# RWKV, experts and a gated recurrence on one core: weights from a surplus made once, sums by accumulating transfers, and a new order of the queues

## The reference

```python
# layer A: RWKV time mix, then channel mix (16 sequences)
k, v, r = (mix(xn, lx, m) @ w for m, w in (key, value, receptance))   # lx: xn shifted by one token
w = exp(time_decay)
# over the tokens, per channel; alpha = beta = 0, eps = -1e30
tau = max(u + k_t, eps); e1 = exp(eps - tau); e2 = exp(u + k_t - tau)
out_t = (e1 * alpha + e2 * v_t) / (e1 * beta + e2)
tau2 = max(eps - w, k_t); d1 = exp(eps - w - tau2); d2 = exp(k_t - tau2)
alpha, beta, eps = d1 * alpha + d2 * v_t, d1 * beta + d2, tau2
x = x + (out * sigmoid(r)) @ w_output
x = x + sigmoid(fr) * (square(relu(fk)) @ f_w_value)      # fk, fr from the second norm
# experts: 8 of them, two for each of the 1024 tokens of sequences 0 and 1
out = scatter_add(gelu(xs @ w1[e]) @ w2[e] * weight) + bias
# layer B: causal convolution of 4 taps, two gates, a linear recurrence, product, RMS norm
h = a * h + scale * (i * conv);  out = rmsnorm(h @ W_out.T) * gamma
# experts again, with the same weights and choice
```

## Time and profile before

| | |
|---|---|
| time, median of three runs | 1257.09 us (1254.84 to 1258.42) |
| span of the profiled execution | 1254.1 us |
| busy: PE, DVE, ACT, POOL | 1186.7, 886.8, 699.7, 537.4 us |
| moved by DMA | 170.78 MB |

### The profile page before, as it was taken

How to read it: one execution, slowest core, us unless ns; L and a number is a source line. 1 busy time by engine, 2 the same in 40 slices (tenths; PEclk the granted TensorE clock), 3 DMA queues, 4 the chain that set the end, 5 groups by cost and what they waited for, 6 DMA issues and landing times. The chain is left out here.

```text
span 1254.1 us, 17087 instructions
## 1 busy us (share of the span) xinstructions
PE 1186.7 (95%) x5812; PEld 927.7 (74%) x5812; DVE 886.8 (71%) x1508; ACT 699.7 (56%) x1100; POOL 537.4 (43%) x514
## 2 busy tenths in 40 slices
PE   5699999999999999999999989999999999999982
PEld 2377787887776868778786768778778678688871
DVE  7989886757587757677889898678567655654336
ACT  2464463555554637455568677567676464554633
POOL 3537652435153062443478637436353602253024
PEclk9799999999999999999999999999999999999997
DMA  7012154646458267575331045657555554656534
GB/s 211 17 34 51 13 164 134 186 122 191 158 138 240 73 162 212 157 202 163 92 85 34 1 105 154 186 158 180 139 146 159 167 167 144 198 140 200 141 100 127
DMA packets 113030, 170.78 MB, mean 136 GB/s; under 512 B 10024, under 2 KB 86576, under 8 KB 112944
## 3 DMA queue, kind: packets, MB, share of 16 engines
q1 hardware_dynamic: 94864, 124.59, 31.2%
q0 software_dynamic: 12320, 39.86, 16.0%
q10 hardware_dynamic: 5760, 5.25, 1.2%
HBM read 138.20 MB, written 16.27 MB: 123 GB/s over the span
## 5 line engine op out<-in xcount | busy, mean ns | idle before, releaser
L2248 PE MATMUL psum<-fwv,hid 128*128 128x256 f32 x1024 | 239.9, 380 | 2.6 <-ACT hid L1225 2.6
L786 POOL TENSOR_TENSOR rstd<-varis,half_neg 128x4 f32<-128x4 f32 x64 | 101.2, 1580 | 282.4 <-DVE varis L3169 191.8
L2248 PEld LDWEIGHTS psum<-fwv,hid 128*128 128x128 f32 x1024 | 190.0, 190 | 32.6 <-issue 4.6
L2289 PEld LDWEIGHTS psum<-xst,ew 128*128 128x128 f32 x1024 | 123.9, 192 | 7.5 <-issue 3.1
L2289 PE MATMUL psum<-xst,ew 128*128 128x128 f32 x1024 | 124.8, 275 | 0.5 <-ACT xst L1306 0.5
L1319 ACT ACTIVATE hidt<-psum 128x512 f32<-128x512 f32 x80 | 47.7, 597 | 133.4 <-PE psum L2289 118.1
L2297 PE MATMUL psum<-ew,hidt 128*128 128x256 f32 x512 | 116.0, 379 | 2.6 <-DMA ew<-in_w 1.9
L1221 ACT ACTIVATE hid<-psum 128x512 f32<-128x512 f32 x128 | 75.5, 593 | 62.4 <-PE psum L2169 40.5
L2297 PEld LDWEIGHTS psum<-ew,hidt 128*128 128x128 f32 x512 | 96.5, 190 | 18.6 <-ACT hidt L1319 2.9
L790 POOL TENSOR_SCALAR xhat<-rows_ring,negmean,rstd 128x256 f32<-128x256 f32 x108 | 96.5, 903 | 24.6 <-PE psum L2158 17.9
L2169 PE MATMUL psum<-xfk_hi,fwk_hi 128*128 128x512 f32 x256 | 93.7, 447 | 1.8 <-issue 1.8
(11 more groups left out here) (303 smaller groups left out, 2496.3 us busy)
## 6 DMA issues: line engine op xcount, KB each, us to landing
ew<-in_w SPq DMA_DIRECT2D x64, 1024.0 KB
ew<-in_w SPq DMA_DIRECT2D x64, 512.0 KB
rows_ring<-bias_rows POOLq DMA_DIRECT2D x28, 512.0 KB, 5.6
rows_ring<-in_x SPq DMA_DIRECT2D x14, 512.0 KB, 6.2
rows_ring<-y POOLq DMA_DIRECT2D x14, 512.0 KB, 5.6
out<-rows_ring SPq DMA_DIRECT2D x14, 512.0 KB, 6.5
rows_ring<-space POOLq DMA_DIRECT2D x12, 512.0 KB
ys_rows<-ys ACTq DMA_DIRECT2D x40, 128.0 KB
```

The source lines that it names most:

```text
L786: pool.tensor_tensor(dst, src, half_neg[:, 0:src.shape[1]], ALU.pow).then_inc(done, 1)
L2248: last = nc.tensor.matmul(rows4[:, k, :], hid[:, j % NHID, k * P:(k + 1) * P], fwv[:, j, :], start=j == 0 and k % 2 == 0, stop=j == FC - 1 ...
L2289: last = nc.tensor.matmul(bank_e[:, j * P:(j + 1) * P], ew1[:, c, at:at + P], xst[:, c, :], start=c == 0, stop=c == DC - 1)
```

## The change

1. A new step `surpluses(b)` overwrites the running maximum by k - decay - top, the key's surplus over the decayed maximum, two passes over 128x512. The decay exponents are then -max(surplus, 0) and min(surplus, 0), two passes over 128x1024 with scalars alone. The exponent of the current weight is the surplus plus (decay + first), capped; that sum, `ahead`, is made once. The first column of `top` is set again for each sequence.
2. `combine(b)` becomes an accumulating transfer of `sf` into the rows, 512 KB, issued by POOL, for all sequences but the last, which keeps the DVE pass (`combine_last`). `receptance(b + 1)`, `third_stats` and the experts' norm wait for it (`summed`).
3. `merge_bias(f, b)` becomes an accumulating transfer of the bias rows, four in all; the bias tile in SBUF and its load go.
4. The queues of all five engines are put into a new order.

The core of the diff, with the places of the new order that the prediction speaks of:

```diff
+            def surpluses(b):
+                for c in range(DC):
+                    dve.wait_ge(tops.sem, tops.count(b, f"m{c}"))
+                    nc.vector.scalar_tensor_tensor(top[:, c, 0:T], kc[:, c, :], decay[:, c:c + 1], top[:, c, 0:T],
+                                                   ALU.subtract, ALU.subtract).then_inc(surplus.sem, 1)
             def weights_now(b):
-                    nc.vector.scalar_tensor_tensor(g[:, c, :], kc[:, c, :], col("first", c), was[:, c, :],
-                                                   ALU.add, ALU.subtract).then_inc(weight_now.sem, 1)
-                nc.vector.tensor_scalar(g[:], g[:], LOGIT_CAP, None, ALU.min).then_inc(weight_now.sem, 1)
+                    nc.vector.tensor_scalar(g[:, c, :], top[:, c, 0:T], ahead[:, c:c + 1], LOGIT_CAP, ALU.add, ALU.min)\
+                        .then_inc(weight_now.sem, 1)
             def weights_decayed(b):
-                    nc.vector.scalar_tensor_tensor(dec[:, 0, c, :], was[:, c, :], decay[:, c:c + 1], top[:, c, 1:T + 1],
-                                                   ALU.add, ALU.subtract).then_inc(decays_in.sem, 1)
-                nc.vector.tensor_tensor(dec[:, 1], kc[:], top[:, :, 1:T + 1], ALU.subtract).then_inc(decays_in.sem, 1)
+                nc.vector.tensor_scalar(dec[:, 0], top[:, :, 0:T], 0.0, -1.0, ALU.max, ALU.mult).then_inc(decays_in.sem, 1)
+                nc.vector.tensor_scalar(dec[:, 1], top[:, :, 0:T], 0.0, None, ALU.min).then_inc(decays_in.sem, 1)
...
+            def combine(b):
+                pool.wait_ge(comb.sem, comb.count(b, "g"))
+                pool.wait_ge(plus_z.sem, plus_z.count(b, "z"))
+                pool.dma_start(rows_of(b).rearrange("p c d -> p (c d)"), sf[:].rearrange("p c d -> p (c d)"), accum_op=ALU.add)\
+                    .then_inc(summed.sem, 16)
...
+            def merge_bias(f, b):
+                pool.dma_start(rows_of(b).rearrange("p c d -> p (c d)"), bias_rows, accum_op=ALU.add).then_inc(biased.sem, 16)
...
             def receptance(b):
-                await_step(act, comb, b - 1, "x")
+                await_step(act, summed, b - 1, "x")
```

More of the change, by code:

```diff
@@ L1518, in turn_5 @@
[L1518 to L1532 removed]
+                square_of(4, 1)
@@ L2578, in turn_5, with turn_6 @@
+                channel_value(4, 4)
+                tile_up(9, 1)
+                freed(ev1, 6, 'e1')
+                outputs(5)
+                channel_key(4, 7, 1)
+                keys(6)
+                tile_down(9)
                 channel_value(4, 5)
-                tile_up(9, 1)
+                tile_in(10)
+                freed(zsum, 5, 'z')
+                transposes_mid(5)
                 channel_value(4, 6)
                 channel_value(4, 7)
-                keys(6)
+            def turn_6():
+                freed(ev2, 5, 'e1')
+                rec_products(1)
+                two_up(10, 0)
@@ L2624, in turn_6 @@
-                freed(ev1, 7, "e1")
-                outputs(6)
-                keys(7)
+                freed(zsum, 6, 'z')
+                transposes_mid(6)
+                tile_up(12, 1)
                 channel_value(5, 5)
-                tile_up(12, 1)
-                channel_key(5, 7, 2)
                 channel_value(5, 6)
-                freed(zsum, 6, "z")
-                transposes_mid(6)
             def turn_7():
                 tile_down(12)
+                channel_value(5, 7)
@@ L3033, in turn_15 @@
                 receptances(14)
                 tile_in(34)
[L3035 removed]
+                channel_value(14, 2)
                 tile_up(34, 0)
[L3037 removed]
+                channel_value(14, 3)
                 tile_up(34, 1)
[L3039 removed]
+                gate_products(13, [(relu, 14, f'f{j}') for j in (2, 3, 4)])
                 tile_down(34)
[L3041 removed]
+                outputs(15)
@@ L3139, in exponent @@
                 step(nc.vector.scalar_tensor_tensor(t, x_, -1.0, x_, ALU.mult, ALU.min))
+                nc.vector.tensor_tensor(ahead[:], decay[:], vec[:, COL["first"]:COL["first"] + DC], ALU.add)\
+                    .then_inc(ahead_made, 1)
             def log_of_sigmoid():
@@ L3486, in experts_rows @@
                                             ALU.add, ALU.mult).then_inc(experts_hat.sem, 1)
-            def merge_bias(f):
-                for c in range(NCH):
-                    await_step(dve, experts_hat, f, f"h{c}")
-                    nc.vector.tensor_tensor(xf[:, c, :], xf[:, c, :], bias[:], ALU.add).then_inc(biased.sem, 1)
             def merge(f, b):
@@ L3807, in turn_8, with turn_9 @@
                 mixed_key(9)
+                mixed_value(9)
+                mixed_receptance(9)
                 residual_mid(8)
                 second_stats(8)
+                gated_input(4)
+                second_differences(8)
+            def turn_9():
                 recur(4)
-                mixed_value(9)
-                mixed_receptance(9)
-            def turn_9():
-                second_differences(8)
                 channel_mix_key(8)
+                channel_mix_high(8)
                 channel_mix_receptance(8)
                 stats_in(10)
-                channel_mix_high(8)
-                weights_ahead(9)
                 channel_mix_low(8)
-                weights_decayed(9)
                 mean_square(4)
                 finish(4)
+                weights_ahead(9)
+                surpluses(9)
+                weights_decayed(9)
+                gated_values(7)
+                merge(0, 0)
+                third_stats(5)
                 beta_sums(9)
```

2127 lines of the change are left out of this document (1074 added, 1053 removed).

## The result

The changed kernel takes 1283.32 us (median of 4 runs, 1281.75 to 1285.3) against 1256.37 (4 runs) of the kernel before on the same chip: a ratio of 1.0214, 95% interval 1.0197 to 1.0231. It is slower by 27 us, outside the range of the prediction (1248 to 1264). The profiled execution has a span of 1279.9 us, 25.8 more than before.

The account below looks back on a forecast made before the run. PE was taken as the bound, busy 1186.7 of 1254.1 us; terms -0.5 + 2.7 + 1.5 - 1 - 1.2 + 0 - 1.9 = -0.4 gave span 1253.7, plus 3.0 carried: 1256.7 us, range 1248 to 1264.

Parts of the forecast that it names:

- What bounds the kernel: Whole kernel: PE busy 1186.7 of 1254.1 us, so lightening DVE alone wins at most 67 idle microseconds.
- The DVE work: All sequences: DVE loses 42 of 887 us: weights 18, channel-mix sums 19, biases 5.5.
- Prologue: Up to outputs(0): PE starts slightly sooner, -0.5 us (bounds -1.7 and +0.5).
- Turn 2 and the start of the experts: Late stats_in(3) stalls PE's transposes, +2.7 us; late combine(1) and norm_power(0) delay the first tile, +1.5.
- Everywhere else: Outside prologue, turns 2, 3, 9, 10 and tail: a shorter DVE queue lies under PE's work.
- Turns 9 and 10: DVE relief gives back 3.7 us, a stall behind combine(7) costs 2.7: net -1 (bounds -4 and +3).
- PE's own time: Whole kernel: PE's own instructions are not changed at all.
- Tile 29 and the loads: Late in the run: -1.2 of tile 29's 2.2 us weight wait; new load order 0 (bounds 0 and +4).
- Tail: transposes_rec(15) takes the place of tile 39's first product and gates start sooner: -1.9 us (bounds -2.4 and 0).
- The third: Rival: transfer delay reaches PE each sequence through receptance, relu and exp on ACT, 8 us; about 1264, chance 0.10.
- The signs: Forecast wrong if PE's idle before 180 us shrinks, or mid-run waits for hid or ew grow to several microseconds.

Follow-up runs that it names:

- e4: Kernel before, old queue order, with only the surplus form of the weights; sums and biases as before: 1257.11 us, ratio 1.0009.
- e7: e4 with the bias also by accumulating transfers; sums stay on DVE, old order: 1257.58 us, ratio 1.0000.
- e3: e7 with the sums also by transfers, so every operation of the change in the old order: 1293.85 us, ratio 1.0294.
- e5: Changed kernel with the channel-mix sums as DVE passes again, right behind gated_values; new order kept: 1285.95 us, ratio 1.0218.
- h4: e7 with the new order through turn 1 and the old order behind it: 1258.15 us, ratio 1.0015.
- h3: e7 with the new order through turn 2 and the old order behind it: 1266.84 us, ratio 1.0081.
- h2: e7 with the new order through turn 8 and the old order behind it: 1275.85 us, ratio 1.0153.
- e1: Changed kernel with picking(0, 1) moved ahead of keep3(4) and residual(4) on POOL in turn 9: 1276.11 us, ratio 1.0159.
- e9: e7 with only the new order of the expert weight loads and the new tail: 1295.28 us, ratio 1.0293.

## Why the prediction was wrong

- **What bounds the kernel.** Right: a lighter DVE is worth nothing by itself. e4 and e7 take 15 and 20 us from DVE and gain 0.
- **The DVE work.** 34.3 us instead of 42. In the old order the operations come close: 15.0 for the weights (18 forecast, e4), 4.8 for the biases (5.5, e7), 20.7 for the sums (19, e3), together 40.5; the other 6.2 are lost with the new order, in which the same DVE instructions are busy longer (e5 against e7: 4.9). The scalar pass over 128x512, taken as 0.42, measured 0.505, and the new weights take 0.75 + 0.75 + 2 x 0.505 + 0.835 + 0.689 + 0.06 = 4.09 us instead of 4.99: 0.9 less where 1.1 was taken. DVE after, by groups (instructions, busy us, mean ns):

```profile
L3305 DVE SCALAR_TENSOR_TENSOR timely<-timely,decay 128x512 f32<-128x512 f32 x32 | 22.6, 746 | 0.0
...
L3314 DVE TENSOR_SCALAR timely<-timely,ahead 128x512 f32<-128x512 f32 x32 | 14.9, 505 | 0.8 <-PE psum L2213 0.8
...
L3321 DVE TENSOR_SCALAR dec<-timely 128x1024 f32<-128x1024 f32 x16 | 13.4, 835 | 1.1
...
L3323 DVE TENSOR_SCALAR dec<-timely 128x1024 f32<-128x1024 f32 x16 | 11.0, 689 | 0.0
```

- **Prologue.** Right in sign: 1.0 us less idle up to 128 us. `outputs(0)` starts 2.4 us sooner (42.03 against 44.40), and its products take 1.2 longer (6.66 against 5.46). h4 shows no gain in the total: what the prologue wins is not kept.
- **Turn 2 and the start of the experts.** Right in mechanism; the size is in part luck. `stats_in(3)` ran 3.5 us later (5.6 was worked out) and the rows of `norm2(2)` ended at 147.6, not at up to 151.5; but PE asked for them at 142.8, not at 145.5 to 146.3. The two errors make up for each other, and the wait of 4.91 us falls within the 3.1 to 6 named. The two terms gave 4.2 = 2.7 + 1.5 and idle time grew by 4.4: 4.91 less the 0.95 that went, and 0.40 at the first gathered tile. What was left out is the clock behind the wait: with it, in e7's surroundings, the part costs 8.7 (h3).
- **Everywhere else.** Wrong: "Everywhere else a shorter DVE queue lies under PE's work" prices the moved steps of turns 3 to 8 at nothing. Idle time there grew by 5.7 us in after, and h2 costs 9.0 over h3. Named waits of after there are 1.36 and 1.82 for POOL's `xhat` and 2.10 for ACT's `hid_rows`; none exists in before. The first two stand in e5 too and belong to the order; the third stands neither in e5 nor in h2, whose sums are DVE's, and comes only with the transfers. Moving steps where PE has no idle time to lose can only be free or cost.
- **Turns 9 and 10.** This step failed worst: -1 forecast with bounds of -4 and +3, +11.3 measured as idle time. I followed `combine(7)` and `merge(0, 0)`, and not `residual(4)`, which the new order puts directly behind `keep3(4)`, whose landing it waits for, with `picking(0, 1)` behind both. e1 prices that at 7.2 us. The stall that I did price, ACT behind `combine(7)`, was 1.67 us at the sequence 8 key products (643.61) where 2.7 was taken. And I took POOL's rows at their short duration, while `norm3(5)` took 9.81.
- **PE's own time.** Taken as fixed ("PE's own instructions are not changed at all"); it grew by 6.1 us. Half of the 2.7 and 5.2 us at 1.2 GHz behind the two new waits is 4.0 of that.
- **Tile 29 and the loads.** The loads cost at most 1.0 us, nearly as said, but only beside the other new orders (e9). Of tile 29's 2.2 us nothing shows at weights; after has 1.0 at another place.
- **Tail.** Right: from tile 38's second product to the gates of sequence 15 it is 16.8 us before (1201.26 to 1218.05) and 14.2 after (1229.30 to 1243.50), 2.6 less where 1.9 was taken, and `transposes_rec(15)` fills the place ahead of tile 39, as described. Before, 1.9 us of that stretch was a wait for tile 39's weights (at 1213.11), priced at 0.7.
- **The rivals.** The third, the transfers' delay on the way to PE in each sequence, names the right kind of cost with too small a price and a minor reader: e3 shows 36 us, and of the waits of PE that e7 lacks the longest come by way of `third_stats` (4.38 through `norm3`, 4.23 and 4.59 through `finish`), with `receptance` at 2.46. But it shows so in the old order. In the changed kernel, which gives the sums room, it is not what made the time longer (after and e5 are not told apart). What did is the order that gives the room. One reading of this, argued and not shown, is that the order was moved to fit the delay, and pays elsewhere.

- **The signs.** Neither sign that was to show the forecast wrong came: PE's idle time up to 192 us grew, and PE's waits for `hid` and `ew` stayed under 2 us each. The loss came where no sign was set, at the gates of turn 9.

Open stay what each of the small waits of turns 3 to 8 comes from, what makes up the rest of turns 9 and later beside e1's 7.2 us (10.1 - 7.2 = 2.9), and whether an order exists that has room for the transfers at the old price.

## What to carry to other kernels

An order written out for several in-order queues is one solution: parts of another put into it cost 36 us (the sums in e3) and 38 (loads and tail in e9), so judge a change of order by each step that is moved, and each wait inside it, for everything queued behind; a transfer that by the program must wait for another one's landing in the same rows holds its whole queue (5.41 us here). Where PE is always busy, relief of another engine is worth nothing, and 5 us more latency on a chain with no room costs at once. Count with each long wait of PE the lower clock that follows it: in e3 the same instructions took 15.5 us longer, of 39.4.

## What the runs showed of the hardware

- The granted clock fell to half (1.2 of 2.4 GHz) within the wait of 9.34 us and was there for 10.2 us, 5.2 of them under products behind the wait. With the waits of 4.91 us (after) and 5.77 us (h3) it was there for 3.4 and 6.8 us, 2.7 and 5.7 of them under products. The same gate products took 2.08 us there and 1.10 a few microseconds on.
- POOL's four scaled rows (128x256) took 9.81 us under DVE scans and two-input passes at 641.09, and 2.41 and 2.60 elsewhere in the same kernel. The Trainium skill ("SBUF — State Buffer", section "Who interferes with whom") states that a DVE instruction with two SBUF inputs contends with a GpSimd instruction that reads SBUF; the duration agrees, and no run here takes the DVE work away to prove it.
- A DVE scalar pass over half the elements (505 ns for 128x512) took 73% of the whole one (689 ns for 128x1024, the cheaper of the two steps).
- The sums by accumulating transfers of 512 KB landed 4.5, 4.9 and 8.4 us (least, median, most) behind their issue, and an issue took 0.96 us of POOL.
